# Forty norm sums as rounded parts: two single-pass products with ones for one fp32 product

## The reference

```python
mu = jnp.mean(x, axis=-1, keepdims=True)
var = jnp.mean(jnp.square(x - mu), axis=-1, keepdims=True)
h = (x - mu) * jax.lax.rsqrt(var + LN_EPS)
h = h * (1.0 + scale[:, None, :]) + shift[:, None, :]
```

## Time and profile before

| | |
|---|---|
| time, median of 3 runs | 2400.38 us (2399.41 to 2405.69) |
| the profiled execution's own time | 2398.59 us |
| its span, first to last instruction | 2396.8 us |
| TensorE busy | 2244.7 us, 94% of the span |
| DVE busy | 1168.9 us, 49% |
| ACT busy | 1033.6 us, 43% |
| POOL busy | 292.5 us, 12% |
| mean granted TensorE clock | 0.98 of full speed |

### The profile page before, as it was taken

How to read it: one execution, slowest core, us unless ns; L and a number is a source line. 1 busy time by engine, 2 the same in 40 slices (tenths; PEclk the granted TensorE clock), 3 DMA queues, 4 the chain that set the end, 5 groups by cost and what they waited for, 6 DMA issues and landing times.

```text
span 2396.8 us, 34593 instructions
## 1 busy us (share of the span) xinstructions
PE 2244.7 (94%) x14034; PEld 1511.1 (63%) x14034; DVE 1168.9 (49%) x2499; ACT 1033.6 (43%) x2425; POOL 292.5 (12%) x246
## 2 busy tenths in 40 slices
PE   5889999999999999999999989999999989999998
PEld 2455555555555687888877756565664668888633
DVE  2345454454457344433443356657587554544322
ACT  2355555444446221111113366657676552222473
POOL 3331122122021001110001010101010110000021
PEclk9889999999999999999999999999999999999999
DMA  8310020000010002110102211011110101100001
GB/s 274 113 40 27 15 64 26 23 23 18 18 40 27 31 27 84 54 61 27 36 6 79 79 53 67 31 63 36 54 36 19 53 1 36 36 1 1 1 18 53
DMA packets 59487, 104.97 MB, mean 44 GB/s; under 512 B 10592, under 2 KB 24560, under 8 KB 59328
## 3 DMA queue, kind: packets, MB, share of 16 engines
q1 hardware_dynamic: 58368, 100.30, 12.6%
q0 software_dynamic: 960, 2.45, 0.3%
HBM read 77.04 MB, written 10.49 MB: 37 GB/s over the span
## 4 chain that ended last, share of the span: by engine, by line
PE 84%; ACT 7%; DVE 6%; POOL 1%; issue 1%; SPq 1%; DMA 1%; DVEq 0%; POOLq 0%; ACTq 0%
PE banks L1213 36%; PE banks L404 22%; PE banks L740 6%; PE banks L732 4%; PE banks L756 4%; ACT sb_Pr L842 2%; PE banks L766 2%; PE banks L265 1%; ACT sb_PT L847 1%; PE banks L906 1%; DVE sb_hN L364 1%; PE banks L630 1%; PE banks L638 1%; DVE sb_Pr L812 1%; PE banks L890 1%
## 5 line engine op out<-in xcount | busy, mean ns | idle before, releaser
L1213 PE MATMUL banks<-sb_HH,sb_Ws 128*128 128x512 f32 x1536 | 490.2, 392 | 12.7 <-DVE sb_HL L1103 7.3
L1213 PEld LDWEIGHTS banks<-sb_HH,sb_Ws 128*128 128x128 f32 x1536 | 289.6, 189 | 76.7 <-issue 16.7
L1213 PE MATMUL banks<-sb_hidH,sb_Ws 128*128 128x512 f32 x1024 | 331.2, 392 | 0.4 <-DVE sb_x L1284 0.4
L842 ACT ACTIVATE sb_Pr<-sb_Pr,sb_nmax 128x512 f32<-128x512 f32 (+4 forms) x512 | 291.6, 576 | 30.9 <-DVE sb_nmax L812 30.8
L1213 PE MATMUL banks<-sb_HL,sb_Ws 128*128 128x512 f32 x768 | 300.0, 391 | 0.0
L847 ACT ACTIVATE sb_PT<-banks 128x512 f32<-128x512 f32 (+2 forms) x320 | 143.5, 496 | 302.6 <-PE banks L740 225.5
L740 PEld LDWEIGHTS banks<-sb_ident,sb_Pr 128*128 128x128 f32 x1536 | 169.7, 142 | 125.5 <-issue 38.9
L819 DVE COPY sb_PT<-banks 128x512 f32<-128x512 f32 (+2 forms) x320 | 168.6, 563 | 163.1 <-PE banks L740 108.7
L740 PE MATMUL banks<-sb_ident,sb_Pr 128*128 128x128 f32 x1536 | 214.2, 282 | 18.2 <-DVE sb_A L830 5.0
L1213 PEld LDWEIGHTS banks<-sb_hidH,sb_Ws 128*128 128x128 f32 x1024 | 192.3, 188 | 44.0 <-issue 2.5
L1213 PE MATMUL banks<-sb_hidL,sb_Ws 128*128 128x512 f32 x512 | 199.4, 389 | 0.0
(11 more groups left out here) (160 smaller groups left out, 3251.7 us busy)
## 6 DMA issues: line engine op xcount, KB each, us to landing
sb_ring<-split_units SPq DMA_DIRECT2D x48, 512.0 KB, 3.3
sb_ropet<-sb_R SPq DMA_DIRECT2D x70, 128.0 KB, 2.0
sb_staged<-in_L_cond_Wfc SPq DMA_DIRECT2D x16, 512.0 KB, 4.6
sb_wada<-in_L_cond_Wada SPq DMA_DIRECT2D x6, 1024.0 KB, 5.5
split_units<-sb_unitpair SPq DMA_DIRECT2D x12, 512.0 KB, 2.9
sb_x<-in_x SPq DMA_DIRECT2D x4, 1024.0 KB, 9.1
sb_staged<-in_L_cond_Wg SPq DMA_DIRECT2D x8, 512.0 KB, 3.7
sb_staged<-in_L_cond_Wu SPq DMA_DIRECT2D x8, 512.0 KB, 4.7
```

The source lines that it names most:

```text
L842: ins = e.activation(prob, prob if s.biased else k.bank(n % 4)[:, 0:s.width(u)], ACT.Exp, bias=s.stat(k, k.nmax, b, u), scale=-1.0 if s.bi ...
L1213: mm = e.matmul(bank, lhsT, rhs, start=i == 0, stop=i == len(mats) - 1)
```

## The change

Every norm's last sum is made in two parts. POOL's third sum now writes `t1parts[:, 1, :]`, the same addresses as `t1[:, 1, :]` but of type float32r: the sum, rounded. The second pair's sum of x goes to `t1[:, 2, :]`, so that its summands stay where they are (for the squares they already were there). DVE then makes what the rounding left out, in two tensor-tensor instructions ("xrest" or "vrest" 0 and 1): the second summand less the rounded sum, plus the first summand, written rounded to `t1parts[:, 0, :]`. TensorE multiplies both parts with ones of type float32r in two single-pass products that add up in the same bank, and waits for DVE's second instruction where it waited for POOL's last. The two DVE operations stand in the beat of POOL's sums, behind them.

The ones are loaded into a tile of their own and copied once by DVE, before all its other queued work; `l_first` counts five transfers instead of six, and the first batch's norm products wait for the copy. Memory: `t1parts` takes the placeholder's addresses, `ones_read` those of `ones`.

```diff
--- before.py
+++ after.py
@@ -230,6 +230,7 @@
 class SideNorm:
     def __init__(s, name, x, h, A, Bias, eps, x_ready, h_free, t_free, rms=False, extra=None, func=None,
                  mod_ready=(), x_loaded=None, high=None, low=None, high_free=()):
         s.x_loaded = x_loaded
@@ -241,7 +242,7 @@
     def beats(s, b):
         squares = [("act", "square", c) for c in range(C)]
         scales = [("dve", "scale", c) for c in range(C)]
-        adds = [("pool", "vsum", i) for i in range(3)]
+        adds = [("pool", "vsum", i) for i in range(3)] + [("dve", "vrest", i) for i in range(2)]
         tail = [adds, [], [("pe", "var", 0), ("act", "log", 0), ("act", "inverse", 0)]]
         if s.rms:
             return [squares] + tail + [scales]
@@ -251,7 +252,7 @@
                     ([("dve", "rest", c - 1)] if c else [])]
         if s.extra:
             ends += [("act", "extra", c) for c in range(C)]
-        return [[("pool", "xsum", i) for i in range(3)], [],
+        return [[("pool", "xsum", i) for i in range(3)] + [("dve", "xrest", i) for i in range(2)], [],
                 [("pe", "mean", 0)] + [op for c in range(C) for op in (("dve", "centre", c), ("act", "square", c))]] \
             + tail + [ends]
 
@@ -260,9 +261,12 @@
 
     def pe(s, k, e, b, kind, i, after):
         bank = s.tab.claim(e, s, b, kind, i, after)
-        for due in after(s.name, b, "xsum" if kind == "mean" else "vsum", 2):
+        if b == 0:
+            e.wait_ge(k.s_ones, 1)
+        for due in after(s.name, b, "xrest" if kind == "mean" else "vrest", 1):
             e.wait_ge(*due)
-        e.matmul(bank, k.ones[:], k.t1[:, 0, :], start=True, stop=True).then_inc(k.done["pe"], 1)
+        e.matmul(bank, k.ones[:], k.t1parts[:, 1, :], start=True, stop=False)
+        e.matmul(bank, k.ones[:], k.t1parts[:, 0, :], start=False, stop=True).then_inc(k.done["pe"], 1)
 
     def pool(s, k, e, b, kind, i, after):
         if kind == "xsum" and i < 2:
@@ -275,7 +279,7 @@
             for key in s.t_free(b):
                 for due in after(*key):
                     e.wait_ge(*due)
-            ins = e.tensor_tensor(k.t1[:, i, :], s.x(b, 2 * i), s.x(b, 2 * i + 1), ALU.add)
+            ins = e.tensor_tensor(k.t1[:, 2 * i, :], s.x(b, 2 * i), s.x(b, 2 * i + 1), ALU.add)
         elif kind == "vsum" and i < 2:
             for due in after(s.name, b, "square", 2 * i + 1):
                 e.wait_ge(*due)
@@ -283,8 +287,7 @@
         else:
             for due in after(s.name, b, kind, 1):
                 e.wait_ge(*due)
-            other = 1 if kind == "xsum" else 2
-            ins = e.tensor_tensor(k.t1[:, 0, :], k.t1[:, 0, :], k.t1[:, other, :], ALU.add)
+            ins = e.tensor_tensor(k.t1parts[:, 1, :], k.t1[:, 0, :], k.t1[:, 2, :], ALU.add)
         ins.then_inc(k.done["pool"], 1)
 
     def act(s, k, e, b, kind, c, after):
@@ -335,7 +338,16 @@
         ins.then_inc(k.done["act"], 1)
 
     def dve(s, k, e, b, kind, c, after):
-        if kind == "centre":
+        if kind in ("xrest", "vrest"):
+            if c == 0:
+                for due in after(s.name, b, kind[0] + "sum", 2):
+                    e.wait_ge(*due)
+                ins = e.tensor_tensor(k.t1[:, 2, :], k.t1[:, 2, :], k.t1parts[:, 1, :].bitcast(F32), ALU.subtract)
+            else:
+                for due in after(s.name, b, kind, 0):
+                    e.wait_ge(*due)
+                ins = e.tensor_tensor(k.t1parts[:, 0, :], k.t1[:, 2, :], k.t1[:, 0, :], ALU.add)
+        elif kind == "centre":
             for due in after(s.name, b, "mean", 0):
                 e.wait_ge(*due)
             for key in s.h_free(b):
@@ -1308,14 +1320,16 @@
         x = sb("x", [P, C, B, T])
         with ExitStack() as scope:
             hNlow = scope.enter_context(nc.sbuf_tensor("sb_hNlow", [P, C, T], F32R))
-            scope.enter_context(nc.sbuf_tensor("sb_t1_offset", [P, C, T], F32))
+            k.t1parts = scope.enter_context(nc.sbuf_tensor("sb_t1parts", [P, C, T], F32R))
             k.rootparts = scope.enter_context(nc.sbuf_tensor("sb_rootparts", [P, 2, T], F32R))
         k.hN = sb("hN", [P, C, T])
         k.t1 = sb("t1", [P, C, T])
         k.Pb = sb("Pb", [P, 2, T])
         k.sd, k.rstd = k.Pb[:, 0, :], k.Pb[:, 1, :]
         k.ident = sb("ident", [P, P])
-        k.ones = sb("ones", [P, P])
+        with ExitStack() as scope:
+            k.ones_read = scope.enter_context(nc.sbuf_tensor("sb_ones_read", [P, P], F32))
+        k.ones = sb("ones", [P, P], F32R)
         k.strip = sb("strip", [P, 32])
         k.lesser = sb("lesser", [P, 1])
         k.freq = sb("freq", [P, 1])
@@ -1400,6 +1414,7 @@
         l_x = [sem(f"l_x{b}") for b in range(B)]
         l_first, l_rope, l_cols, l_cond = sem("l_first"), sem("l_rope"), sem("l_cols"), sem("l_cond")
         l_ada = [sem(f"l_ada{i}") for i in range(3)]
+        l_ones, k.s_ones = sem("l_ones"), sem("s_ones")
         k.s_angle, l_wo0 = sem("s_angle"), sem("l_wo0")
         l_w = [sem(f"l_w{i}") for i in range(2)]
         l_w3 = sem("l_w3")
@@ -1464,7 +1479,7 @@
         n_cols = len(COLS) + 2
         BLOCKS = ADA * P // D
         ada = Ada(cond, lambda j: wada[j % 3], lambda j: (l_ada[j % 3], 16 * (j // 3 + 1)), ada_rows, sel[:], mod, modb,
-                  [float(j in (0, 2, 3, 6, 7, 10)) for j in range(BLOCKS)], combs, (l_first, 16 * 6),
+                  [float(j in (0, 2, 3, 6, 7, 10)) for j in range(BLOCKS)], combs, (l_first, 16 * 5),
                   (l_cols, 16 * n_cols), (l_cond, 16))
         angles = Angles()
 
@@ -1979,7 +1994,7 @@
             for b in range(B):
                 e.dma_start(k.pos[32 * b:32 * b + 32, :], a["pos"][b].partition_broadcast(32)).then_inc(k.l_pos, 16)
             e.dma_start(k.ident[:], a["ident"]).then_inc(l_first, 16)
-            e.dma_start(k.ones[:], a["ones"]).then_inc(l_first, 16)
+            e.dma_start(k.ones_read[:], a["ones"]).then_inc(l_ones, 16)
             e.dma_start(sel[:], a["sel"]).then_inc(l_first, 16)
             e.wait_ge(s_zero, 4)
             for name, t0, n in MODB:
@@ -2003,6 +2018,8 @@
             e.memset(eps6[:], 1e-6).then_inc(s_zero, 1)
             e.memset(cond[:], 0.0).then_inc(s_zero, 1)
             e.memset(modb[:], 0.0).then_inc(s_zero, 1)
+            e.wait_ge(l_ones, 16)
+            e.tensor_copy(k.ones[:], k.ones_read[:]).then_inc(k.s_ones, 1)
             engine(e, "dve", 0, len(phases))
 
         @block.scalar
```

## The result

The changed kernel takes 2454.36 us, median of four runs (2450.33 to 2455.22), against 2399.89 (2399.13 to 2405.69) for the kernel before in the same session: 1.022 times as long, 95% interval 1.0205 to 1.0235. That is 54.5 us, not the 29 forecast. It lies 14 us above the 2440 to which the prediction gives its chance, and 10 above the 2444 at which it lets the range end. The profiled execution took 2450.33 us with a span of 2448.5.

A forecast was written before the change was run, and what follows sets the result against it. TensorE, busy 94% of the span, was taken as the bound. Stalls of 48.1 us, less a tenth 43.3, less 14.3 saved, gave +29.0 us and 2428; forecast 2408 to 2440 (chance 0.63), wider range 2405 to 2444.

The forecast's parts named there:

- the port: DVE's pair and POOL's next instruction sharing SBUF access: at least two places, 0.65 us each, 1.3 us counted.
- The product: 40 norm products on TensorE, each 0.406 us shorter: 17 us taken, 14.3 of it reaching the end.
- The stalls: TensorE made late by DVE's pair and its wait for POOL's last sum: 48.1 us, less a tenth, 43.3.
- The one place that I counted at nothing: Layer 0 attention, mean of third batch: a 4.2 us loss, taken as swallowed by TensorE's 7.0 us stand later.
- the sum itself: Stalls: start 3.3, layer 0 12.7, layer 1 6.0, layer 2 attention 15.6, feed-forward 5.6, last layer 3.6, port 1.3; 48.1 us.
- The price of 0.65: DVE's wait for one POOL instruction, less overlap, in us; from three two-operand DVE instructions taking 4.20 us beside POOL.
- The sentence on the Trainium skill in the prediction: DVE with two SBUF inputs and POOL exclude each other: every pair with POOL work behind the sum pays up to 1.3 us.
- Savings win: Rival: the order's lead makes up DVE's 3 to 5 us stops, leaving the 14.3 saved; about 2384 us, chance 0.07.
- Swallowed: Rival: two thirds of the 48.1 us of delays go into existing waits, the rest cancels the saving; about 2400, chance 0.13.
- Product not shorter: Rival: ones and parts still take two passes each, so the 14.3 us saving is missing; 2442 us, chance 0.06.
- DVE as the bound of both attentions: Rival: every stop costs in full in layers 0 and 2, 20 us more; about 2448 us, chance 0.11.
- The signs: In the trace: L265 near 392 ns, new DVE instructions near 690, attention stretches 6 to 15 us longer each, 850 to 1350 unchanged.

The follow-up runs named there:

- product alone: The changed kernel without DVE's pair: both single-pass products read POOL's rounded sum with halved ones, rest left out; 2391.63 us against 2402.31 for the kernel before.
- two beats later: The changed kernel with DVE's pair moved into the product's own beat, just ahead of it; 2495.3 us against 2401.9 for the kernel before.
- layer 0 as before: The changed kernel with layer 0's eight norm sums as in the kernel before, the other 32 changed; 2438.43 us, 1.0147 of the kernel before.
- product waits too: As pair with its wait, and the norm product waits for the second DVE instruction; 2438.2 us against 2401.9 for the kernel before.
- POOL makes the rests: The changed kernel with both instructions of the pair made by POOL behind its last sum, not by DVE; 2431.9 us, 1.0127 of the kernel before.
- pair with its wait: As pair without its wait, and the first of the two DVE instructions waits for POOL's last sum; 2433.93 us, 1.0122 of the kernel before.
- one beat later: The changed kernel with DVE's pair moved into the empty beat between POOL's sums and the product; 2431.8 us, 1.0118 of the kernel before.
- pair without its wait: As product alone, plus two DVE instructions on a constant in the pair's place, waiting for nothing; 2402.53 us, 0.9997 of the kernel before.
- POOL where free: POOL makes the rests at 17 sums with over 2.6 us before their product, other 23 as in the kernel before; 2398.24 us against 2402.08.
- the control: As product alone, plus forty unused single-pass TensorE products at five places in layers 0 and 1; 2391.21 us against 2404.24 for the kernel before.

## Why the prediction was wrong

The direction was right, and so was the mechanism of the stalls; the size was half, because two terms of the sum were wrong: the length of all other TensorE work, put at nothing, and the port. The kernels stand in a row:

| kernel | us | step |
|---|---|---|
| before | 2402 | |
| product alone | 2392 | -11 |
| and a pair's time on DVE | 2403 | +11 |
| and DVE's wait for POOL | 2434 | +31 |
| and the product's wait for DVE | 2438 | +4 |
| and the real operands (the change) | 2454 | +16 |

**The product.** Forecast -14.3; measured -11 by itself and -11.3 by the pairing. The rate was right at the thirteen places where the product is 0.39 to 0.40 us shorter, not at the others, and the 4.2 us that became idle time are more than the discount by TensorE's share of the chain. The prediction calls the fp32 product two passes; by its rows that is two instructions of 0.43 us each, against 0.227 for a single-pass one.

**The stalls.** Forecast 43.3 after the discount; measured 39.9 of added idle time. Place by place, from TensorE's starts at the same operations: layer 0, variance of the third batch 7.0 late for 6.5 forecast; the mean of the last batch 3.6 for 2.6; layer 2's third batch 3.5 for 3.1; the first norm before layer 2's feed-forward part 1.9 for 2.3. In the second feed-forward part the mean product lost 1.5 and not 3.0, and one of the two variances nothing. Some of the nearness of the two sums is luck: the 39.9 hold the 4.2 of the saving that became idle time, some 9 of the port, and a place that the forecast left out. The stages: layer 1 5.2 for 6.0, layer 2's attention 13.6 for 15.6, its feed-forward part 3.3 for 5.6, layer 3 3.2 for 3.6. At the start the cast of the ones moved DVE's first step from 11.42 to 12.14, 0.7 as forecast:

```profile
11.99 0.23 DVE L2022 CAST sb_ones<-sb_ones_read 128x128 fp32r<-128x128 f32 x1 [10.74 <-DMA sb_ones_read<-in_ones]
12.14 0.42 DVE L79 CAST sb_A<-sb_A 128x512 f32<-128x512 int32 x1
```

The one place that I counted at nothing, the mean of layer 0's third batch, was priced better than it was excused. TensorE stands 3.70 us there (4.2 in the bound) and is 6.3 later 3 us on. The stand of 7.01 some 15 us later shrinks to 4.17 only, and behind it 3.3 of the 6.3 are left. An idle stretch ahead swallows a delay only if the delayed work isn't what that stretch waits for; here the transfer it waits for is itself late, since DVE's rotary instruction behind it starts at 170.34 for 165.85. That the transfer was late because the rope product that feeds it was, I argue from the order of the queue and didn't test.

**The step that failed** is the sum itself: "3.3 + 12.7 + 6.0 + 15.6 + 5.6 + 3.6 + 1.3 = 48.1 us of stalls", less the saving, and nothing else. It took each stall for its own length and all other TensorE work for as long as before, without a reason. The trace shows 23.1 us more pitch in work that the change doesn't touch, 19.8 of them in layer 0, where the granted clock goes from 0.96 to 0.90; the 40 us of idle time came with 33 us more of clock withheld. The earlier trace rows had the clue: 0.95 in layer 0 and 1.00 in layer 2. Layer 0 lost 19.8 on 14.6 of idle time, layer 2's attention 1.9 on 13.6. The last column of the next table is the clock withheld while other TensorE work ran, idle time and norm products left out: over the runs it goes with the pitch.

| kernel | more clock withheld | more pitch of other work | more withheld during it |
|---|---|---|---|
| two beats later | 47.8 | 41.4 | 37.9 |
| the change | 30.7 | 23.1 | 24.1 |
| layer 0 as before | 29.0 | 21.8 | 23.9 |
| product waits too | 25.6 | 18.3 | 20.1 |
| POOL makes the rests | 25.6 | 14.0 | 16.9 |
| pair with its wait | 23.9 | 24.1 | 22.7 |
| one beat later | 15.4 | 9.1 | 8.4 |
| pair without its wait | 3.4 | 9.1 | 5.6 |
| POOL where free | 0 | 0.2 | 0.8 |
| product alone | -1.7 | -1.7 | 0.3 |

(Here the clock is summed over the paired operations, and each line is one profiled execution.) The change's 23.1 us are thus covered by the clock. The third line from below doesn't fit: the pair without its wait has 7.7 of its 9.1 in layer 0, where its clock was as before, so DVE's occupation alone can lengthen TensorE's pitch there. That a lower clock costs its time is shown by the kernel before alone: over 45 executions its granted clock went from 0.981 to 0.976 and its time from 2397.83 to 2407.78, 12 us more withheld and 10 us longer, and in between the two keep in step (0.9 us for each us withheld). The changed kernel's four have 0.965 to 0.967, below all of these. That a stand of TensorE makes the clock fall is shown by the table of the three places above, where the edits put stands in and take them out. The rest of the trace agrees: in the changed kernel 19 of the 21 falls of the clock after 150 us come within 5 us of the beginning of a stand of over 1.2 us, though about half of the 35 such stands have no fall behind them.

**The port** was the second term mis-sized: 1.3 forecast, 16 measured with all that follows from it (which overlaps with the idle time and the pitch above). Both of its factors were too small. The price of 0.65 came from three instructions of the earlier trace rows taken as one mean, but the first of them was over before POOL began; the two beside POOL took 1.80 and 1.64 us, 1.0 to 1.1 above their 0.69, as the seven L345 do now. And instead of two places it was nine, eight with a long L345 and one with a long L349 alone: in the kernel before, too, eight of POOL's 40 last sums have another POOL instruction at once behind them. L345 takes 883 ns over 40, 0.2 above its 0.69: 8 us of DVE time, not 1.3, two thirds of it before 450 us, straight in the path of the copies that TensorE waits for there. The sentence on the Trainium skill in the prediction gave up to 1.3 us for each pair with a POOL instruction behind it; it was nearer than the sum.

**The rivals.** Savings win: no; the product alone shows what they were worth. Swallowed: no. Product not shorter: no. DVE as the bound of both attentions, 2448, is nearest in its number and wrong in its cause: DVE is busy 225 of 360 us in layer 2 as before, and that stage lost less than forecast. **The signs** that I named came out in part: 80 new DVE instructions, but with means of 883 and 740 ns and not near 690; 80 products, but with 553 and 454 ns and not near 392, and 40.2 us of busy time for 47.4 and not half; 850 to 1350 us unchanged; nine products waiting for DVE in place of five; and, not named, the clock of 110 to 310 us, 0.90 for 0.95.

## What to carry to other kernels

In an engine that works in order, an instruction is to be put where its input is there and its reader isn't due yet: the wait cost 31 us where its instructions cost 11, the pair one beat later 23 less, two beats later, just ahead of its reader, 41 more. Count TensorE's stalls at more than their length, above all where the granted clock is below 1.00 already. Here they cost 20 us on 15 in layer 0 and 2 on 14 in layer 2's attention, but with the pair two beats later 12 on 20 in that same stage, so the second pair of numbers is no rule. A DVE instruction with two SBUF operands that waits for POOL meets POOL's next instruction if one stands at once behind: look at what follows the sum in POOL's queue before putting it there, and count one place for each (here nine of 40, 1.0 us at most of them).

## What was not expected of the hardware

- An L345 beside a POOL rope product took 1.73 us and one without took 0.69; two reduces of one SBUF operand in the same place took 0.70 each, and tensor-tensors with one operand in PSUM (L356) 0.68. It isn't DVE's work beside POOL's that is slow, but work with two operands from SBUF.
- In layer 0 the granted clock fell from 0.96 to 0.90 though TensorE was still busy 87% of the time (294.89 of 340 us), 90% before. The two levels, 1.2 and 2.4 GHz, lie behind this mean: between these two, 0.90 is a fifth of the stretch at the lower one. A single stand of 1.94 us was followed by 13.7 us at the lower level, and the same eight products took 5.73 us there and 3.70 with the stand filled. The Trainium skill, "TensorE: Matmul & The Clock Gate", section "What's actually happening", says that a monitor sets the gate by how busy TensorE has been of late; the table of clock and pitch above agrees but for the line named there.
- 40 idle products of 128x512, 9 us by 0.227 each, cost nothing that could be measured, with stalls around them (2452.44 for 2454.36) and without (2391.21 for 2391.63). In the control each eight of them put TensorE back by 1.4 to 2.7 us where they stand; behind the first two places a later wait swallowed it.
